# Recommendation tower on one core: five fields by selection, dot products in two column tiles, a ring of 28 rows

## What is computed

```python
e = jnp.stack([tbl_0[ids[:, 0]], ..., tbl_31[ids[:, 31]]], axis=1)      # 2048 x 32 x 256
iu, ju = jnp.triu_indices(32, k=1)
z = jnp.einsum('bnd,bmd->bnm', e, e)[:, iu, ju]                          # 2048 x 496
h = jnp.concatenate([z, dense_ctx], axis=1)                              # 2048 x 512
h = jnp.maximum(h @ W_top1 + b_top1, 0.0)                                # 512
h = jnp.maximum(h @ W_top2 + b_top2, 0.0)                                # 256
y = h @ W_top3                                                           # 1
```

## Time and profile before

| | |
|---|---|
| median of 3 runs | 623.67 us (623.08 to 625.48) |
| the profiled execution, device time | 627.5 us |
| its span, first to last instruction | 625.7 us |
| TensorE busy | 563.3 us, 90% |
| TensorE weight loads busy | 555.9 us, 89% |
| GpSimd busy | 436.8 us, 70% |
| VectorE busy | 365.1 us, 58% |
| ScalarE busy | 285.1 us, 46% |
| granted TensorE clock, mean share of full speed | 0.988 |

### The profile page before, as it was taken

One profiled execution on the slowest core, in us unless ns is written; L12 is line 12 of the kernel. 1 busy time (PEld: TensorE's weight loads), 2 busy tenths in 40 slices (PEclk: granted clock), 3 DMA queues, 4 the chain that ended last, 5 costly groups with the idle time before them and its releaser, 6 DMA issues.

```text
span 625.7 us, 11900 instructions
## 1 busy us (share of the span) xinstructions
PE 563.3 (90%) x4864; PEld 555.9 (89%) x4864; DVE 365.1 (58%) x802; ACT 285.1 (46%) x503; POOL 436.8 (70%) x454
## 2 busy tenths in 40 slices
PE   0269999999999999999999999999999899998973
PEld 0259999989999999999999999999999899998973
DVE  3165847657483856658483857658483575835330
ACT  0173545544363544545364544545354354545330
POOL 6788777777777777777777777777777777775000
PEclk9999999999999999999999999999999899999997
DMA  7982343455344644455343643455343743354000
GB/s 174 230 272 74 113 116 113 115 78 151 107 115 114 114 116 113 116 80 149 107 119 111 115 114 115 115 79 148 110 119 108 112 118 105 110 88 107 2 1 0
DMA packets 35600, 69.79 MB, mean 112 GB/s; under 512 B 15590, under 2 KB 20198, under 8 KB 35046
## 3 DMA queue, kind: packets, MB, share of 16 engines
q0 software_dynamic: 21504, 58.75, 37.7%
q1 hardware_dynamic: 14042, 10.28, 6.9%
HBM read 68.98 MB, written 0.01 MB: 110 GB/s over the span
## 4 chain that ended last, share of the span: by engine, by line
POOL 45%; PE 29%; issue 15%; DMA 5%; DVE 4%; ACT 1%; DVEq 0%
POOL rows L234 45%; PE gram_ps L270 12%; PE sel_ps L324 6%; PE tr_ps L249 5%; DMA rows<-in_tbl,ids_sb 4%; PE gram_ps L292 4%; PE gram_ps L302 2%; DVE sel_low L424 1%; DVE onehot L437 1%; PE gram_ps L281 0%; DVE emb_t L366 0%; DVE dots L383 0%; ACT dots L383 0%; DVE dots_t L445 0%; PE gram_ps L310 0%
## 5 line engine op out<-in xcount | busy, mean ns | idle before, releaser
L234 POOL DMA_INDIRECT rows<-in_tbl,ids_sb x448 | 436.1, 973 | 137.5 <-issue 135.0
L270 PE MATMUL gram_ps<-emb_t 128*128 128x124 f32 x2048 | 240.2, 276 | 0.3 <-DVE y_sb L472 0.3
L270 PEld LDWEIGHTS gram_ps<-emb_t 128*128 128x128 f32 x2048 | 235.2, 193 | 0.6 <-issue 0.4
L366 DVE COPY emb_t<-tr_ps 128x512 f32<-128x512 f32 x112 | 127.8, 1141 | 67.7 <-PE tr_ps L249 66.8
L383 ACT COPY dots<-gram_ps 32x124 f32<-32x124 f32 x256 | 96.0, 375 | 132.6 <-PE gram_ps L270 130.4
L249 PE MATMUL tr_ps<-ident,rows 128*128 128x128 f32 x896 | 120.8, 280 | 37.3 <-DMA rows<-in_tbl,ids_sb 37.3
L366 ACT COPY emb_t<-tr_ps 128x512 f32<-128x512 f32 x112 | 128.2, 1145 | 54.1 <-PE tr_ps L249 52.7
L249 PEld LDWEIGHTS tr_ps<-ident,rows 128*128 128x128 f32 x896 | 104.6, 146 | 39.6 <-DMA rows<-in_tbl,ids_sb 20.1
L324 PE MATMUL sel_ps<-onehot,sel_high 125*128 125x256 f32 x512 | 126.4, 287 | 7.2 <-DVE emb_t L373 6.3
L383 DVE COPY dots<-gram_ps 32x124 f32<-32x124 f32 x256 | 94.6, 370 | 55.3 <-PE gram_ps L270 52.7
L324 PE MATMUL sel_ps<-onehot,sel_low 125*128 125x256 f32 x512 | 124.0, 283 | 0.0
(11 more groups left out here) (19 smaller groups left out, 108.2 us busy)
## 6 DMA issues: line engine op xcount, KB each, us to landing
rows<-in_tbl,ids_sb POOLq DMA_INDIRECT x448, 2.8
sel_ids<-in_ids_by_field SPq DMA_DIRECT2D x32, 128.0 KB, 3.5
emb_t<-in_tbl SPq DMA_DIRECT2D x4, 896.0 KB
w_sb<-in_W_top SPq DMA_DIRECT2D x1, 1024.0 KB
w_sb<-in_W_top SPq DMA_DIRECT2D x1, 512.0 KB
emb_t<-in_tbl SPq DMA_DIRECT2D x4, 104.0 KB
packed<-in_dense_ctx SPq DMA_DIRECT2D x16, 8.0 KB
ids_sb<-in_ids SPq DMA_DIRECT2D x1, 240.0 KB, 3.0
```

The source lines that it names most:

```text
L234: pool.indirect_dma_start(out=rows[g % RING][:, j, :], out_offset=None, in_=tables[f], in_offset=bass.IndirectOffsetOnAxis(ap=ids_sb[:, t, ...
L270: last = nc.tensor.matmul(gram_out[k][:, g, :], four.rearrange("p s f -> p (s f)"), four[:, :, 0:firsts], start=(h == 0), stop=(h == D_HAL ...
L366: copy(emb_t[t % PAIR][:, h, :, at[0]:at[-1] + 1].rearrange("p (g s) f -> p f s g", s=QUAD), tr_ps[h][g % 2][:].rearrange("p f (s g) -> p ...
```

## The change

- A fifth field (20) is selected instead of gathered. A tile has 27 gathered rows, in six quads of four and one of three: 432 gathers, 40 selection jobs in place of 32.
- The ring is counted in single rows: 28 of them in place of 32.
- `gram` splits each group of four samples into two products of two samples: 64 columns of weights, 62 streaming columns, written to partitions 0 to 63 or 64 to 127. A fill is 8 groups (4 fills a tile), and `dots_copy` makes four copies of 8 x 31 values per fill.
- Eleven quads are turned before the first dots, seven of tile 0 and four of tile 1, with the five first jobs between them. From then on six quads are turned in an odd period and eight in an even one, so quads stand four ahead of where they stood. Jobs are placed between the fills.
- The tables are loaded one after another, each behind the landing of a quad, into space of their own; the one-hot matrix has one buffer, handed over in halves; the context is loaded once and copied by DVE (one small copy per tile).
- `layer3` has its operands exchanged, so the result is one row of 128 values on one partition. SP stores it per tile as one row of 512 bytes, and the buffer is a part of `hid2_t`, so DVE's copy behind layer 2 waits for the store before.

```diff
-SELECTED = (22, 24, 27, 31)
+SELECTED = (20, 22, 24, 27, 31)
 SELECT_CHUNKS = 8
-RING = 8
+RING = 28
 SPRAY = 16
+TILED = 2
+EARLY = 2
+AHEAD = 4
...
-    bank_groups = 4
+    bank_groups = 8
...
+    turns_at_start = quads + AHEAD
+    turns_odd, turns_even = 6, 8
+
+    def quad_turned(t, at):
+
+        pairs_before, odd = divmod(t - 1, PAIR)
+        g = turns_at_start + pairs_before * (turns_odd + turns_even) + odd * turns_odd + at
+        return g if g < len(every_quad) else None
...
-        rows = [sbuf(f"rows{r}", [P, QUAD, width]) for r in range(RING)]
+        rows = sbuf("rows", [P, RING, width])
...
-        y_sb = sbuf("y_sb", [P, PAIR])
+        y_sb = hid2_t[0:1, 0, :]
+        ctx_sb = sbuf("ctx_sb", [P, tiles, ctx_width])
...
-        onehot = [sbuf(f"onehot{s}", [select_rows, SELECT_CHUNKS, pair_cols], f32r) for s in range(2)]
+        onehot = sbuf("onehot", [select_rows, SELECT_CHUNKS, pair_cols], f32r)
...
-            def load_ctx(t):
-                wait(sp, turned[1], t)
-                sp.dma_start(packed[:, pairs_of_fields:], dense_ctx[t * P:(t + 1) * P, :]).then_inc(ctx_loaded, DMA)
-
-            def store_y(p):
-                sp.wait_ge(y_copied, (p + 1) * PAIR)
-                with nc.allow_non_contiguous_dma(reason="the results, a word per sample"):
-                    sp.dma_start(y[p * pair_cols:(p + 1) * pair_cols, :].rearrange("(u p) o -> p (u o)", p=P),
-                                 y_sb[:]).then_inc(y_stored, DMA)
...
+            load_table(0)
+            for n in range(1, n_sel):
+                sp.wait_ge(rows_loaded[(n - 1) % quad_sems], rows_landed(n - 1) * DMA)
+                load_table(n)
...
+                sooner = 2 if t % PAIR else 1
+                for job in jobs(t + 1)[:sooner]:
                     load_sel_ids(*job)
-                if t < tiles:
-                    load_ctx(t)
-                if t % PAIR == 0:
-                    store_y(t // PAIR - 1)
-            sp.wait_ge(y_stored, DMA * (tiles // PAIR))
+                sp.wait_ge(y_copied, t)
+                sp.dma_start(y[(t - 1) * P:t * P, :].rearrange("s o -> o s"), y_sb).then_inc(y_stored, DMA)
+                for job in jobs(t + 1)[sooner:]:
+                    load_sel_ids(*job)
+            sp.wait_ge(y_stored, DMA * tiles)
...
+                for slot, place in zip(slots(g), places(k)):
+                    j = t * n_rows + place - RING
+                    if j >= 0 and quad_of_row(j) >= freed:
+                        freed = quad_of_row(j) + 1
+                        pool.wait_ge(transposed[1], freed)
...
-                        four = emb_t[u][:, h, s:s + QUAD, :]
-                        last = nc.tensor.matmul(gram_out[k][:, g, :], four.rearrange("p s f -> p (s f)"),
-                                                four[:, :, 0:firsts], start=(h == 0), stop=(h == D_HALVES - 1))
+                        for c in range(0, QUAD, TILED):
+                            own = emb_t[u][:, h, s + c:s + c + TILED, :]
+                            last = nc.tensor.matmul(gram_out[k][c * fields:(c + TILED) * fields, g, :],
+                                                    own.rearrange("p s f -> p (s f)"), own[:, :, 0:firsts],
+                                                    start=(h == 0), stop=(h == D_HALVES - 1))
...
-                    last = nc.tensor.matmul(mlp_ps[0][:, 0:1], hid2_t[:, i, :], w3_sb[:, i:i + 1],
+                    last = nc.tensor.matmul(mlp_ps[0][0:1, 0:P], w3_sb[:, i:i + 1], hid2_t[:, i, :],
...
+            def odd_period(t):
+                early = (jobs(t) + [None] * EARLY)[:EARLY]
+                def turning(at):
+                    for h in range(D_HALVES):
+                        transpose(quad_turned(t, at), h)
+                gram(t - 1, 0)
+                select(early[0], 0)
+                turning(0)
+                gram(t - 1, 1)
+                select(early[0], 1)
+                turning(1)
+                gram(t - 1, 2)
+                gram(t - 1, 3)
+                turning(2)
+                for h in range(D_HALVES):
+                    select(early[1], h)
                 turn(t - 1)
+                turning(3)
                 if t == 1:
                     pe.wait_ge(weights_loaded, 5 * DMA)
                 layer1(t - 1)
+                turning(4)
+                layer2(t - 1)
+                transpose(quad_turned(t, 5), 0)
+                layer3(t - 1)
+                transpose(quad_turned(t, 5), 1)
+            def even_period(t):
+                late = (jobs(t) + [None] * 4)[:4]
+                def turning(at):
+                    for h in range(D_HALVES):
+                        transpose(quad_turned(t, at), h)
+                gram(t - 1, 0)
+                gram(t - 1, 1)
+                turning(0)
+                gram(t - 1, 2)
+                gram(t - 1, 3)
+                turning(1)
+                for h in range(D_HALVES):
+                    select(late[0], h)
+                turn(t - 1)
+                turning(2)
+                layer1(t - 1)
+                turning(3)
+                layer2(t - 1)
+                select(late[1], 0)
+                layer3(t - 1)
+                select(late[1], 1)
+                turning(4)
+                for h in range(D_HALVES):
+                    select(late[2], h)
+                turning(5)
+                select(late[3], 0)
                 turning(6)
+                select(late[3], 1)
                 turning(7)
             pe.wait_ge(ident_ready, 1)
+            first_jobs = jobs(0)
+            for g in range(turns_at_start):
+                for h in range(D_HALVES):
+                    transpose(g, h)
+                for job in first_jobs[g - 2:g - 1] if g >= 2 else []:
+                    for h in range(D_HALVES):
+                        select(job, h)
...
+            next_jobs = first_jobs[1:] + jobs(1)[:1]
+            for g in range(turns_at_start):
+                emb_copy(dve, 0, copy, g)
+                if 1 <= g <= n_sel:
+                    split_table(g - 1)
+                for job in next_jobs[g - 2:g - 1] if g >= 2 else []:
+                    for half in range(2):
+                        build_onehot(job, half)
```

More of the change, by code:

```diff
@@ L340, in period @@
                 turn(t - 1)
-                turning(5)
+                turning(3)
                 if t == 1:
@@ L539 @@
+            for g in range(turns_at_start):
+                if g < n_sel:
+                    high_table(g)
+                emb_copy(act, 1, copy, g)
+                if 2 <= g < 2 + n_sel:
+                    copy_selected(0, jobs(0)[g - 2])
+            act.wait_ge(weights_loaded, 5 * DMA)
+            for t in range(1, tiles + 1, PAIR):
+                odd_period(t)
+                even_period(t + 1)
 def kernel(**inputs):
```

362 lines of the change are left out of this document (206 added, 156 removed).

## The result

The changed kernel takes 600.43 us (median of 4 runs, 599.15 to 602.57) against 624.58 (623.08 to 627.96) for the kernel before, measured beside it: a ratio of 0.961 with an interval of 0.956 to 0.966. Its profiled execution took 599.15 us, with a span of 597.6. The forecast was 596.0 (585 to 630) and a span of 598.0. Medians and ratios are of undisturbed executions; in the second experiment two of ten, the profiled one among them, were disturbed (625.1 and 624.9 us, where the fastest took 614.6), so only one wait is read from its profile. Each experiment has the kernel before measured beside it, and its median moved between 624.6 and 629.4 us from one set of runs to the next; so a difference between two medians of different sets can be off by up to 5 us, and the ratio to before is the safer figure.

What follows compares the result with a forecast made beforehand. POOL and TensorE bound the kernel before; afterwards POOL, its last gather starting at 556.8 us, plus the end gives a span of 598.0. (598.0 + 1.8) x 0.9939 = 596 us; own range 586 to 608, stated range 585 to 630.

Steps and rivals of the forecast that it cites:

- What bounds: Kernel before: POOL and TensorE neck and neck, 70.1 and 71.3 us per pair of tiles; a gain needs both to fall.
- the gain of POOL: Field 20 removes 16 gathers at a 1.2526 us step, leaving 432 and 67.6 us per pair; 17 us less of POOL.
- The dots: TensorE's dots, G per pair: both column tiles overlap, 28 ns per record, G = 14.3; full or nearly full overlap, chance 0.70.
- the rival: Serial tiles: column tiles take turns, G = 28.6, TensorE bounds alone; 70 + 524 + 58 = 652, about 650 us; chance 0.11.
- the prediction's floor rival: Dots: a half-size record costs as much as a full one, G = 57.1, 876 us; 62 ns gives about 674; chance 0.08.
- The holds: POOL's gathers stopped by five table splits and one-hot runs behind four of them: 14 us taken, range 6 to 19.
- the prediction's rule: On DVE, table splits and what follows one without a gap stop POOL's gathers; one-hot instructions without a split held none.
- the one-hot term: Four runs of eight one-hot instructions behind splits add up to 8.7 us of hold at most, less for gaps left.
- The end: After the last gather's start at 556.8: landing, chain of tile 14, dots and chain of tile 15, store; span 598.0, +/-4.
- the factor 0.9939: Turns span into time: before's median of 623.67 us against its profiled execution of 627.5 us.
- TensorE's spare time: TensorE needs 62.5 us per pair against POOL's 67.6, so it waits for rows some 5 us per pair in steady state.
- Hidden as forecast: DVE's copies and one-hot work stay under 50 us per pair, single-buffer waits within 2 us on TensorE; table loads don't slow POOL.

Runs made afterwards that it cites:

- the second experiment: Kernel before with only the dots split into two column tiles, old field split, ring and order; 619.37 us, 0.988 of before.
- the third run: Changed kernel with four selected fields as before, 448 gathers; 620.63 us, 0.990 of before.
- the fifth run: Kernel before with DVE's copy of a quad moved from ahead of a table split to behind it; 627.09 us beside 625.73 for before.
- first: Changed kernel with one loop moved, so all products of one column tile come before the other's within a fill; 671.78 us, 1.073 of before.
- seventh: Changed kernel with 14 and 17 unused matmuls ahead of the turning of dots in tiles 14 and 15; 595.85 us, 0.952 of before.
- tenth: Changed kernel with six fields, ring of 12, one quad of lead, filling matmuls, third and fourth jobs' ids loaded before the weights; 588.07 us, 0.937 of before.
- fourth: Changed kernel with quads turned one ahead instead of four; 585.52 us, 0.936 of before.
- ninth: Changed kernel with quads turned one ahead and filling matmuls before the last two turnings; 581.85 us, 0.924 of before.
- eleventh: Changed kernel with a ring of 12 rows in place of 28, nothing else; 616.01 us, 0.979 of before.
- the eighth: Changed kernel with six selected fields, a ring of 12 rows and quads turned one ahead; 600.81 us, 0.962 of before.

## Why the prediction was right, and where it was off

**What bounds, and the gain of POOL: right.** The step stayed at 1.25 us, 16 gathers fewer are 20.0 us, and with four fields (the third run) 18 to 20 us were gone. That POOL was a bound before is borne out: TensorE relieved alone brought 7 us (the second run). That TensorE was one as well rests on its 70.4 busy us in a pair of 71.3; the fifth run agrees, but delayed TensorE too, so no run relieved POOL alone.

**The dots: the disputed price was right.** The forecast took full overlap, 28 ns per record, G = 14.3. Measured are 30.3 ns, G = 15.5. The bound of 55.8 for serial tiles came out as 55.2, and the rival as a real kernel at 671.78. The forecast gave it 650; its sum was 652, the span measured 669.8. Its start was 75.3 us instead of 70, a pair 75.6 instead of 74.8, the rest 65.1 instead of 58. So it was priced too low in all three terms, the end by most, 7 us. The start, 70 against 74.7 in the changed kernel as well, left out TensorE's wait for the third job's ids. What the prediction did not say is that the overlap hangs on neighbours in program order lying in different tiles. The Trainium skill (TensorE: Matmul & The Clock Gate, "The mechanism") says that weight loads overlap running matmuls only when the row group differs; both column tiles stand on all rows, and 30.3 ns against 55.2 speaks against it. Its 62 ns per matmul ("Back-to-back issue gap") can be neither confirmed nor refused here: a record takes half of that, but these f32 matmuls leave two records each (2048 matmuls, 4096 records), and a matmul of the program takes 60.6 ns. What the prediction's floor rival made of it, 62 ns per record, did not come.

**The holds: mis-sized, 14 against 7.9.** The 14 were 10 for five splits and 4 for the one-hot runs behind them. The splits took 6.5: a gather was held from its own start on, and four of the five started only 0.9 to 1.1 us into the split. The one-hot runs took 1.4, once. In DVE's timeline three of the four runs first waited, 1.61, 15.25 and 0.40 us, for a free matrix or for the ids, and the gather beside the split ended in the gap. Here are the last two splits:

```profile
56.27 2.27 DVE L510 TENSOR_TENSOR sel_low<-sel_raw,sel_high 125x2048 fp32r<-125x2048 f32 x1
58.94 2.56 DVE L525 TENSOR_SCALAR onehot<-sel_ids,row_numbers 125x256 fp32r<-125x256 int32 x8 [0.40 <-PE sel_ps L359]
...
62.37 2.29 DVE L510 TENSOR_TENSOR sel_low<-sel_raw,sel_high 125x2048 fp32r<-125x2048 f32 x1
64.57 2.19 DVE L525 TENSOR_SCALAR onehot<-sel_ids,row_numbers 125x256 fp32r<-125x256 int32 x8
```

A gap of 0.40 us was enough: the gather of 56.37 ended at 59.35, 0.81 us behind the split. Without a gap the gather of 63.41 ended at 66.88, with the one-hot instructions. So far this is the prediction's rule, that what follows a split without a gap prolongs the hold. But the rule is only half right. With a gap of 0.27 us or more no hold was prolonged in any run. Without one it was prolonged in five cases (here, in the kernel before and in the first, seventh and tenth run), and in six it was not (one each in the fourth, ninth, tenth and eleventh run, two in the eighth). In the run with six fields and a ring of 12, DVE's rows and POOL's beside them:

```profile
65.07 2.29 DVE L510 TENSOR_TENSOR sel_low<-sel_raw,sel_high 125x2048 fp32r<-125x2048 f32 x1
67.28 2.52 DVE L525 TENSOR_SCALAR onehot<-sel_ids,row_numbers 125x256 fp32r<-125x256 int32 x8
```

```profile
65.33 2.85 POOL L264 DMA_INDIRECT rows<-in_tbl,ids_sb  x1 [0.30 <-issue]
```

That gather ended at 68.18, 0.82 us behind the split, with one-hot instructions running. What decides between the two is not known. The prediction said that some gaps would be left; that three of four were left is the larger part of the one-hot term's error. POOL was 6.4 us sooner than forecast: 550.44, not 556.8.

**The end: mis-sized, 41.2 against 47.2.** From the last gather's start, forecast against measured: to DVE's dots transposition 4.6 and 6.5; chain of tile 14 11.3 and 14.1; dots of tile 15 7.9 and 8.6; their last copies 2.2 and 2.4; chain of tile 15 12.7 and 13.7; store 2.5 and 1.7. The first is not the last quad's landing, as forecast. TensorE had begun the last two fills of tile 14's dots at 550.49, behind the quad before the last, and turned the last quad only after them, at 554.37; DVE then waited 1.11 us for ACT's copies of the second fill, which take 0.60 us each and not the 0.5 taken. The prediction took this stretch to hang on the last quad alone. The chains are the clock. Before, tile 14's chain had quads between its steps; the prediction took 11.1 us from there though it had itself noted that the last quad moved ahead of the chain. Without those quads TensorE idles between its steps and layer 1 takes 6.58 us. In the seventh run, at full clock, both chains take 11.2 us, against 14.1 and 13.7, and the end is 5.4 us shorter, which shows it.

**The two errors cancelled, which is luck.** A span of 598.0 was forecast and 597.6 measured, with 6.4 us too much for POOL and 6.0 too little for the end. The time missed by 4.4 us (0.7%) for a third reason: the factor 0.9939 took over that before's profiled execution was slower than its median, and the changed kernel's (599.15) was faster than its own. So the time says less of the steps than it seems.

**TensorE's spare time: too large in the forecast.** 5 us per pair were expected; the window has 3.6 idle, of which 2.5 are waits for rows, and TensorE's own pace in the fourth run, 64.4 us, leaves 3.2. The sixth field shows how close it is: one job more and TensorE is the bound.

**Hidden as forecast:** the one-hot buffer and the copies, and, as far as POOL goes, the table loads. Not foreseen was the 15.25 us wait for the ids, which the ring hid: the lead of its 28 rows, which the forecast counted on between quads, was needed at the start, and is worth 11 us by the ratios and 15.6 by the medians.

## What to carry to other kernels

When two engines run neck and neck, relieve both: here TensorE alone brought 7 us, both together 24. Put neighbouring small matmuls into different column tiles, in program order, and not one tile's after the other's. Work that is turned ahead of need is free in the middle and dear at the end: ask of the last item what was moved behind its landing, and whether the engine that is left runs bare there at the lower clock.

## What the hardware showed that was not expected

Matmuls of half the width cost 30.3 ns per record when neighbours lie in different column tiles and 55.2 when they lie in the same one. A two-input VectorE split of 2.3 us from SBUF to SBUF holds the gather that starts beside it, to about 0.8 us behind its end where nothing prolonged it, and not the one under way, which took its usual 0.94 or 0.95 us. A one-input instruction of 1.2 us held five gathers to 1.50 to 1.97 us, two of them already under way. One-hot instructions right behind a split prolonged the hold in five cases of eleven, to a gather of 7.11 us at most. In a bare chain of 4, 32, 16 and 4 records, with copies between them, the granted clock of the stretch was 0.76 to 0.77; 28 to 34 records of no use ahead of it brought it back to 1.00 and about 5 us with it. A result row of 512 bytes on one partition was stored in 1.7 us, where a word per sample took 8.7.
